# Second attention layer on one core: scores and maxima on quarters of TensorE's columns in quads 1, 14 and 15

## The reference, cut to what matters

```python
def _L1_xattn_ref(x, cond, wq, bq, wkv, bkv, wp, bp):
    q = _qdq(x) @ _qdq(wq).T + bq            # 8-bit rounding, kept in floats
    kv = cond @ wkv.T + bkv
    k, v = jnp.split(kv, 2, axis=-1)         # 16 heads x 16 dimensions
    ...
    attn = jax.nn.softmax(jnp.einsum('bnhd,bmhd->bhnm', q, k) * scale, axis=-1)
    o = jnp.einsum('bhnm,bmhd->bnhd', attn, v).reshape(B, N, C)
    return _qdq(o) @ _qdq(wp).T + bp
```

## Time and profile before

| what | us |
|---|---|
| median of 3 runs (lowest, highest) | 811.05 (809.56, 811.33) |
| the profiled execution: its time | 809.53 |
| its span, from first to last instruction | 807.6 |
| TensorE busy | 751.5 (93%) |
| VectorE busy | 566.8 (70%) |
| ScalarE busy | 383.5 (47%) |
| mean granted TensorE clock | 0.987 |

### The profile page before, as it was taken

How to read it: one execution, slowest core, us unless ns; L and a number is a source line. 1 busy time by engine, 2 the same in 40 slices (tenths; PEclk the granted TensorE clock), 3 DMA queues, 4 the chain that set the end, 5 groups by cost and what they waited for, 6 DMA issues and landing times.

```text
span 807.6 us, 13086 instructions
## 1 busy us (share of the span) xinstructions
PE 751.5 (93%) x5026; PEld 425.8 (53%) x5027; DVE 566.8 (70%) x1290; ACT 383.5 (47%) x562; POOL 197.8 (24%) x208
## 2 busy tenths in 40 slices
PE   7999899979989889789999999999999999899996
PEld 3445677856556556544444455554455554345434
DVE  3967988633455765687788787767787777887814
ACT  2101434445423233236666666556665566564670
POOL 1397322323721311210400504100505002200000
PEclk9999999999999999999999999999999999999999
DMA  9300001105589143144083391630491810550000
GB/s 294 138 0 1 1 1 27 57 1 185 113 146 138 62 60 47 22 60 79 1 145 40 117 135 16 142 55 2 150 116 62 115 23 1 117 69 14 1 2 13
DMA packets 32473, 55.90 MB, mean 69 GB/s; under 512 B 11572, under 2 KB 20532, under 8 KB 31509
## 3 DMA queue, kind: packets, MB, share of 16 engines
q1 hardware_dynamic: 32408, 55.04, 34.6%
HBM read 42.56 MB, written 12.46 MB: 68 GB/s over the span
## 4 chain that ended last, share of the span: by engine, by line
PE 64%; DVE 23%; issue 6%; POOL 3%; ACT 2%; DMA 1%; SPq 0%; DVEq 0%; POOLq 0%; ACTq 0%
PE ps L1111 12%; PE ps L1000 12%; PE ps L1090 9%; PE ps L888 5%; PE ps L898 5%; DVE small L1679 5%; PE ps L944 3%; PE ps L964 3%; POOL r L623 2%; PE ps L814 2%; PE ps L857 2%; PE ps L845 2%; DVE small L1629 1%; DVE r L1598 1%; DVE r L1605 1%
## 5 line engine op out<-in xcount | busy, mean ns | idle before, releaser
L1679 DVE TENSOR_REDUCE small<-ps 128x1 f32<-128x400 f32 (+1 forms) x512 | 286.0, 573 | 81.5 <-PE ps L1000 75.4
L1490 ACT ACTIVATE r<-ps 128x1024 f32<-128x1024 f32 (+1 forms) x208 | 212.6, 1024 | 89.0 <-PE ps L1090 86.1
L1000 PE MATMUL ps<-r 96*128 96x400 bf16 (+1 forms) x512 | 171.0, 341 | 13.7 <-DVE small L1679 10.9
L651 POOL TENSOR_TENSOR r<-r 128x401 bf16<-128x401 f32 (+3 forms) x96 | 87.8, 949 | 204.3 <-ACT r L1331 203.2
L1111 PE MATMUL ps<-r 128*17 128x256 f32 (+1 forms) x1664 | 130.7, 386 | 2.3 <-ACT r L1490 2.0
L1090 PE MATMUL ps<-r 99*128 99x256 bf16 (+1 forms) x832 | 125.8, 273 | 0.0
L1000 PEld LDWEIGHTS ps<-r 96*128 96x128 bf16 x512 | 49.5, 97 | 125.8 <-DVE small L1679 92.6
L1090 PEld LDWEIGHTS ps<-r 99*128 99x128 bf16 (+1 forms) x832 | 81.4, 99 | 31.5 <-issue 9.3
L944 PE MATMUL ps<-r,hT 128*128 128x512 f32 (+1 forms) x160 | 68.4, 559 | 0.0
L898 PE MATMUL ps<-wkvT,r 128*128 128x256 f32 (+1 forms) x208 | 57.0, 392 | 0.0
L1111 PEld LDWEIGHTS ps<-r 128*17 128x17 f32 (+1 forms) x1664 | 27.7, 95 | 52.0 <-issue 41.4
(11 more groups left out here) (199 smaller groups left out, 966.9 us busy)
## 6 DMA issues: line engine op xcount, KB each, us to landing
r<-kscr SPq DMA_DIRECT2D x96, 200.1 KB, 8.9
kscr<-r SPq DMA_DIRECT2D x24, 400.2 KB, 3.5
r<-in_ctx_dram SPq DMA_DIRECT2D x4, 1601.0 KB, 6.7
r<-qscr SPq DMA_DIRECT2D x24, 128.0 KB, 4.9
r<-in_wo_dram SPq DMA_DIRECT2D x1, 2048.0 KB, 13.5
r<-in_gu_dram SPq DMA_DIRECT2D x1, 2048.0 KB, 7.7
qscr<-qpart SPq DMA_DIRECT2D x24, 64.0 KB, 1.7
x<-in_x_dram SPq DMA_DIRECT2D x1, 1024.0 KB, 5.3
```

The costliest lines, as they stand in the source:

```text
L651: last = nc.gpsimd.tensor_tensor(into[:, a:a + n], kf[s][:, a:a + n], of[:, a:a + n], ALU.subtract)
L1000: mm(bank(ca % 2)[:, 0:m], qst[0:SROWS, h, q0:q0 + P], kst[0:SROWS, s % 2, h % HALF, a:a + m], start=True, stop=True).then_inc(mx_mm, 1)
L1490: fn(pr[i % 3][0:n, :], bank(2 + 2 * (i % 2), 2)[0:n, :], ACT.Exp, scale=SCALE1)\
L1679: v.tensor_reduce(mxc[quad % 2][:, n:n + 1], bank(ca % 2)[:, 0:m], AX_X, ALU.max).then_inc(mx_rdy, 1)
```

## The change

Two constants are added, and in the steps of the three quads each product of `scores` and each chunk of `max_scores` is written as four products on 32 stationary columns, each with the same moving operand as before and each writing its own 32 partitions (in step 12, with 65 keys, `scores` makes three: 32, 32 and 1). The semaphore is raised by the last of them. Nothing else changes: not the operands, not the banks, not the order of the steps.

```diff
+QUARTER = P // 4
+QUARTERED = (1, 14, 15)
...
-            def max_scores(quad, n):
+            def max_scores(quad, n, width=P):
...
-                mm(bank(ca % 2)[:, 0:m], qst[0:SROWS, h, q0:q0 + P], kst[0:SROWS, s % 2, h % HALF, a:a + m],
-                   start=True, stop=True).then_inc(mx_mm, 1)
+                for r in range(0, P, width):
+                    last = mm(bank(ca % 2)[r:r + width, 0:m], qst[0:SROWS, h, q0 + r:q0 + r + width],
+                              kst[0:SROWS, s % 2, h % HALF, a:a + m], start=True, stop=True)
+                last.then_inc(mx_mm, 1)
...
-                    last = mm(bank(2 + 2 * (i % 2), 2)[0:n, k * LQ:(k + 1) * LQ],
-                              kst[0:SROWS + 3, s % 2, h % HALF, kt * P:kt * P + n],
-                              qst[0:SROWS + 3, h, b * LQ:(b + 1) * LQ], start=True, stop=True)
+                    width = QUARTER if quad in QUARTERED else P
+                    for r in range(0, n, width):
+                        z = min(r + width, n)
+                        last = mm(bank(2 + 2 * (i % 2), 2)[r:z, k * LQ:(k + 1) * LQ],
+                                  kst[0:SROWS + 3, s % 2, h % HALF, kt * P + r:kt * P + z],
+                                  qst[0:SROWS + 3, h, b * LQ:(b + 1) * LQ], start=True, stop=True)
...
+                    width = QUARTER if quad in QUARTERED else P
...
-                            max_scores(*maxima.pop(0)[1:])
+                            max_scores(*maxima.pop(0)[1:], width)
```

## The result

The changed kernel took 804.75 us (median of 8 runs, 802.27 to 809.03) against 809.97 us for the kernel before (median of 8): a ratio of 0.9945, with a 95% interval of 0.9922 to 0.9967. It is faster, by 5.2 us between the medians.

What follows compares the result with a forecast made beforehand. TensorE, 93% busy, was taken to lose 0.10 us at each of two width changes a step in quads 1, 14 and 15. 1.1 + 1.5 + 0.2 - 0.5 = 2.3 us less gave 808.8 us, range 807.0 to 812.8.

Steps and rivals of the forecast that it cites:

- The mechanism: Steps of quads 1, 14 and 15: two changes of width on TensorE, about 0.20 us a step, go; chance 0.60.
- Quad 1: Five two-chunk steps from 1.44 to 1.25 us, one gaining 0.36, the "k" step +0.2; sum -1.1 us.
- the step of the key products: Quad 1: the "k" job stays full width, so four switches instead of two, +0.2 us.
- Quad 14: Five of six two-chunk steps gain 0.36 us, 1.8 in all, with 0.3 given back at the end; -1.5 us.
- step 3: Quad 14: the two-chunk step beside VectorE's work on the output, said to gain nothing.
- the step of `shift`: End of quad 14: waits for VectorE's short instructions, so its gain of four switches is only waiting; 0.3 us given back.
- Quad 15: TensorE's need falls to 0.90 us a step, but ScalarE holds 1.10; -0.2 us in all.
- The price of quarters: All three quads: cost of quarter products beyond their stream, 0.004 us a set of four, +0.5 us in all.
- the late last quarter: The semaphore comes with the fourth product, so 1.02 us becomes 1.04 where chunks bound; included in the 0.5 us.
- Side by side only in part: Rival: quarters do not run fully side by side; 0.02 us more a set eats the gain, 811.1 us; chance 0.20.
- The clock: Rival: TensorE's clock falls once more, costing about 1.5 us, so the gain is 0.8: 810.3 us; chance 0.10.
- Instructions too slow: Rival: TensorE's instructions come too slowly, deciding from 25 ns each on; 5.2 us more, 816.3 us; chance 0.10.

Runs made afterwards that it cites:

- by_neighbour: Against the kernel before: quarters in all sixteen quads, but chunks full width from a step's key, value, up, down or expert products on; 829.38 us, ratio 1.0234.

## Why the prediction was right and wrong

*The mechanism was right.* Two changes of tile size a step cost 0.10 us each and go only when chunks and scores are both quarters of the weigh's size. Moving them (chunks alone), doubling them (scores alone) and replacing them by another size (halves) all gave what a price for each change of size gives. The Trainium skill ("TensorEngine Tiling (Array Packing)", Tiling Modes) says that changing the tiling mode drains the engine; the 0.10 us at each change agree with it, and so does a price between 64 and 32 columns.

*Quad 1: the sum was right, in part by luck.* -1.1 forecast, -1.12 measured. But the step of the key products grew by 0.39 us (3.13 to 3.52), where I had +0.2 for two changes more: I did not have the 0.10 us that each key product loses between its passes. Steps with two chunks gained more than forecast, 0.22 us (1.44 to 1.22) where I had 0.19, and 0.44 in the one behind a step with three, where I had 0.36.

*Quad 14: nearly.* -1.5 forecast, -1.73 measured. The six steps with two chunks gained 2.1 us, not 1.8; step 3, in which I had nothing, gained 0.25. Five steps with three chunks grew by 0.03 each, and the step of `shift` gave back 0.2 instead of 0.3.

*Quad 15: the step that failed.* I had ScalarE hold the step at 1.10 us, from two exponentials in a row, and -0.2. It measured -0.65. The 1.10 us were TensorE's own: 0.54 from scores to weigh and 0.56 from weigh to scores, with both changes in them. The kernel before has two exponentials that follow faster, at the end of quad 14, at 1.93 - 1.02 = 0.91 us:

```profile
768.04 1.93 ACT L1490 ACTIVATE r<-ps 65x1024 f32<-65x1024 f32 x2
```

The timeline of quad 15 after, without its loads:

```profile
775.75 0.63 PE L1118 MATMUL ps<-r 128*17 128x256 f32 x8
775.95 1.94 ACT L1498 ACTIVATE r<-ps 128x1024 f32<-128x1024 f32 x2 [0.25 <-PE ps L1097]
776.20 0.62 PE L1097 MATMUL ps<-r 99*32 99x256 bf16 x16
777.02 0.63 PE L1118 MATMUL ps<-r 128*17 128x256 f32 x8 [0.20 <-ACT r L1498]
777.47 0.62 PE L1097 MATMUL ps<-r 99*32 99x256 bf16 x16
...
778.13 1.02 ACT L1498 ACTIVATE r<-ps 128x1024 f32<-128x1024 f32 x1 [0.24 <-PE ps L1097]
```

Two exponentials follow at 1.94 - 1.02 = 0.92 us, and ScalarE idles 0.24 us before the next; steps of 0.92 and 1.26 us alternate where it was 1.10 and 1.18. What bounds is a loop over two steps: exponential (775.95 to 776.97), weigh (777.02), the scores behind it (777.47), the next exponential but one (778.13), 2.18 us. The weigh inside it fell from 0.56 to 0.45, so the loop fell by 0.11, which is 0.05 us in each step. My sign for the forecast, even steps at 1.10 us with ScalarE without gaps, did not come.

*The price of quarters: the second term that was mis-sized.* I took +0.5 us. Sixteen quarter scores cost no more than four whole ones, and a step with two chunks came out at 1.22 us, below the 1.24 that I had without any price. Only the 0.03 us in each step with three chunks may be the late last quarter, 0.15 us in quad 14. With -2.8 before that term and quads 14 and 15 at their measured size, the sum is 3.5.

*The rest of the error is not the kernel.* 1.0 of the 5.2 us is the clock's luck in eight runs, and the remaining 0.7 lies within what the runs leave open. The forecast also started from a median of 811.05 us for the kernel before, which came out at 809.97. My range put the low end 1.8 us below the forecast, though its own term for one fall of the clock was 1.5 us and the runs shown spread over 1.8; with 3.7 us less than 811.05 the time would have lain inside it.

*The rivals.* Side by side only in part: refuted by the timeline. The 2.38 times for three tiles that the Trainium skill gives ("TensorE: Matmul & The Clock Gate", Part 3) do not describe these sets of four, which run in the time of one. The clock: a fall came and one went, by chance. Instructions too slow: not in these quads, where quad 14 takes 840 in 19.6 us. But that rival was closer than I made it. Its limit is not the pace of issue but the fetch of instructions behind DMA traffic, and with quarters in quads 2, 4, 8 and 12 it costs more than all gains.

## What to carry to other kernels

Count the changes of tile size along TensorE's program, not its products. Here narrow work among wide work paid 0.10 us in and 0.10 out, and 0.10 more inside a float32 product of full width that followed narrow work; quartering a wide product to match its neighbours was free in TensorE's time. Mind a remainder of another size, such as the one key beside 64. Quarters are paid for in instructions, so use them where DMA is quiet, and look for idle stretches put down to "issue" while the DMA share is at 1. Before you take a limit from two instructions in a row, see whether the second waited for another engine. Where runs spread by the granted clock, sum the windows of the stretches that changed, or compare runs at equal clock, before believing a median.

## What the runs showed of the hardware

- Sets of four quarter matmuls in bfloat16 started within 0.01 to 0.02 us, one set per 0.11 us for 256 columns: the time of one whole product.
- An exponential of 1024 columns, 1.02 us long, started 0.91 to 0.92 us after the one before, in both kernels.
- Between products of 1, 17 and 32 columns there was no price; between those and 64 or 128 columns each change cost about 0.10 us.
- The instruction blocks of TensorE share the DMA engines with data: with the engines at a share of 1, the next block came 14.7 us after the last instead of 5.7. With the key copies cut from 200 to 50 KB, by_neighbour's blocks came 5.4 and 5.9 us apart in the same quad.
